# One more tile per batch multiplied with a whole table instead of gathered, and the softmax exponent of a slot moved behind a stretch of passes

## The chip, the cores and the metric

The kernel runs on one core of a Trainium2 chip, as one program. The metric is the device time of one execution in microseconds (us); lower is better. Engine names in the profile: PE is TensorE (PEld its weight loads), DVE is VectorE, ACT is ScalarE, POOL is GpSimd, SP is SyncE.

## The reference

For each of 16 batches of 512 tokens of width 128, a graph layer is followed by an attention layer with 8 heads, whose keys and values come from a memory of product keys. Per token and head, two similarity vectors over 128 sub-keys are cut to their top 16, their 256 sums again to the top 16, and the softmax of these weighs 16 rows of a table of 128 x 128 rows:

```
x = x + gnn(layernorm(x), adj)
q = x' @ Wq * D**-0.5                        # x' = layernorm(x)
scores, idx = top_k(sim, 16)                  # two sides of 128 keys
final_scores, pk_idx = top_k(all 256 sums, 16);  final_scores = softmax(final_scores)
k = einsum(final_scores, keys_table[ind]);  v = einsum(final_scores, values_table[ind])
out = softmax(causal(q k^T)) v;   x = x + concat(out) @ Wo
```

## The kernel before, in words

**Tiling.** A batch is 4 tiles of 128 tokens. Seven heads (`GH`) are gathered and one (`DENSE`, the eighth) is not. The work of a batch is laid out in 28 slots n = 4h + t, one per gathered head h and tile t. `schedule` runs a first batch, a loop of 14 and a last batch. Each engine has its own hand-ordered program over the same slots, tied by semaphores.

**A gathered tile.** DVE finds the rows (`rank`, `pairs_of`, `best_of`, `one_hot`, `hot_rows`, `sum_rows`, `even`, `lay`), always one head ahead and in pairs of tiles: `rank` for a pair in the slot with even t, the rest in the slot with odd t. At the end of that odd slot `take_laid` writes `rows` (L1131) and `spread`. POOL then issues 16 indirect DMAs for each tile (L397) into one of three buffers `got`. It waits for `rows_ready` and for `combined` of the tile three back. PE combines the rows with 32 matmuls (L659), which wait for the gathered rows. ACT copies the result to `kv` (L721, as all copies).

**The attention of the slot.** PE turns the keys (`key_transpose`, L544), ACT copies them, PE makes the scores (L548), DVE negates and masks them (`negate`, L1239), ACT takes the exponential (`exponent`, L826), PE turns the probabilities (`prob_transpose`, L554), ACT copies, PE multiplies with the values (L560), ACT copies, PE projects (L566), DVE adds (`add`, L1254, L1259).

**The dense head.** Its keys and values are made by multiplying a 128 x 16384 matrix of weights with the whole table. The matrix is built a piece at a time in *passes*. In a pass ACT makes four exponentials (`raise_`, L786), DVE cuts them by rank with four instructions (`weigh`, L1222), PE turns the four (`turn`, L506), ACT copies them (`take_wideT`), and PE multiplies (`multiply`, L520: four products, eight instructions in the trace). ACT is two passes ahead, DVE one, and `multiply` two behind `turn`. A pass serves 2 keys of 2 tiles, so two halves of 64 passes make 128 per batch. SP loads the table in chunks of 8 keys, 1 MB, into two buffers (`load_chunk`, L334); a chunk lasts 4 passes, and its load waits until the chunk two back is used up. Before chunk 5, SP stores the previous batch's output and waits until it has landed (L325, L327).

**Where the passes stand.** The plans `MIDDLE` (all batches but the last) and `ENDING` give each slot five counts, the passes of its five stretches. Stretch 3 and stretch 4 lie between scores and `prob_transpose` on PE; on ACT, `exponent` stands between them; stretch 5 comes before the values. Preparing a half of the dense head takes DVE four slots (`rank_dense`, `pairs_dense`, `best_dense`, `count_dense`, `norm_dense`; table `PREP`), and counting its ranks four *sets* of 16 instructions (`hit`, L1186) and of 16 PE matmuls (`add_hits`, L496), one slot each (table `HITS`), then `take_sum`. The dense head's own attention is interleaved in four slots.

**Order in a slot on ACT**, which the change touches:

```
k = passes(b, k, w[2], first, last)
exponent(slot, t)
k = passes(b, k, w[3], first, last)
take_probT(slot, t)
```

Of the kernel before, what the change touches and what calls it, by code (L numbers as in the profile page):

```python
# [21 lines left out]
SLOTS = GH * T  # L22
TOKENS = P // TOPK
# [6 lines left out]
HALF_PASSES = NKEYS // 2  # L30
PASSES = 2 * HALF_PASSES
CHUNK = 4
KEYS = 2 * CHUNK
CHUNKS = PASSES // CHUNK

# [15 lines left out]
ENDING = [  # L51
    FIVE, FOUR, FOUR, THREE,
    SEVEN, FIVE, SIX, FOUR,
    SEVEN, FIVE, SIX, FIVE,
    SEVEN, FIVE, SIX, FIVE,
    SIX, FIVE, SIX, FIVE,
    SEVEN, FIVE, SIX, FOUR,
    NONE, NONE, NONE, NONE]
# [7 lines left out]
PREP = {1: 0, 0: 20}  # L66
HITS = {1: {4: 0, 5: 1, 6: 2, 7: 3}, 0: {23: 0, 24: 1, 25: 2, 26: 3}}
# [24 lines left out]

def got_no(n):

    return n % 3 if n < SLOTS - 1 else 1


def got_back(n):

    return next(d for d in range(1, 6) if got_no((n - d) % SLOTS) == got_no(n))  # L100

# [15 lines left out]
def program(nc, x, adj, w_msg, w_upd, bias, wqpk_t, keys_t, wq, table, dense, wo, out):  # L117
# [85 lines left out]
    sim_d = sb("sim_d", [P, T, SIDES * NKEYS])  # L203
    top_v_d = sb("top_v_d", [P, 2, SIDES, TOPK])
# [9 lines left out]
    z_inv = sb("z_inv", [P, T])  # L214
    put = sb("put", [P, 2, SIDES, TOPK])
    hits = [sb(f"hits{i}", [P, TOPK, NKEYS], BF16) for i in range(2)]
    count_sb = sb("count_sb", [P, 2, NKEYS])
    rank1 = sb("rank1", [P, T, NKEYS])
    shift1 = sb("shift1", [P, T, NKEYS])
# [79 lines left out]

    def past(n):  # L300

        return max(n, 0) if isinstance(n, int) else n
# [13 lines left out]
    def _(sp):  # L316
# [48 lines left out]
    def _(pool):  # L365
# [19 lines left out]
        def batch(b, first=False, last=False):  # L385
            for n in range(SLOTS):
                h, t = n // T, n % T
                slot = b * SLOTS + n
                pool.wait_ge(rows_ready, slot + 1)
                pool.sem_inc(held, 1)  # L390

                if not (first and n < 3):
                    pool.wait_ge(combined, slot - (got_back(n) - 1))
                    pool.sem_inc(held, 1)
# [11 lines left out]
    def _(pe):  # L406
# [39 lines left out]
        def front(b, h, first=False, last=False):  # L446

            f = b * GH + h
            if h == 0:
                pe.wait_ge(xnT_copied, b * 2 + 2)  # L450
                pe.wait_ge(sim_d_copied, b * 2 + 1)
            elif h == 4 and not last:
                pe.wait_ge(xnT_copied, b * 2 + 3)
            elif h == 5 and not last:
                pe.wait_ge(x_used, b + 2)
            elif h == 2:
                pe.wait_ge(sim_d_copied, b * 2 + 2)
                if not first:
                    pe.wait_ge(added_d, b * 4)
            elif h == 3:  # L460
                pe.wait_ge(q_d_copied, b + 1)
            elif h == 6:
                pe.wait_ge(added_d, b * 4 + 2)
# [12 lines left out]
        def front_dense(b, half, f):  # L476
# [3 lines left out]
            for t in (2 * half, 2 * half + 1):  # L480
                last = pe.matmul(front_ps[1][:, (t % 2) * 256:(t % 2 + 1) * 256], x2nT[:, t * P:(t + 1) * P],
                                 w_sim[:, DENSE * 256:(DENSE + 1) * 256], start=True, stop=True)
# [7 lines left out]
        def add_hits(b, half, g):  # L490

            m = b * 8 + (half * 4 + g)
# [16 lines left out]
        def multiply(b, k):  # L509
            m = b * PASSES + k  # L510
            half, r = k // HALF_PASSES, k % HALF_PASSES
            if r % CHUNK == 0:
                c = k // CHUNK
                pe.wait_ge(tab_loaded[c % 2], b * (CHUNKS // 2 * 16) + (c // 2 + 1) * 16)
            if r == 0:
                pe.wait_ge(kv_d_copied, b * 4 + 2 * half)
            pe.wait_ge(wideT_copied, m + 1)
            for u in range(2):
                for v in range(2):
                    mm = pe.matmul(dense_ps[:, v * 2 * D:(v + 1) * 2 * D],  # L520
                                   wideT[k % 2][:, (2 * u + v) * P:(2 * u + v + 1) * P],
                                   tab[(k // CHUNK) % 2][:, (2 * k + u) % KEYS, :],
                                   start=(r == 0 and u == 0 and v == 0), stop=(r == HALF_PASSES - 1 and u == 1),
                                   skip_group_check=True)
# [15 lines left out]
        def key_transpose(a, t):  # L540
            pe.wait_ge(kv_copied, a + 1)
# [26 lines left out]
        def key_transpose_dense(c, tile, f):  # L568

            pe.wait_ge(kv_d_copied, c - tile + (tile // 2 * 2 + 2))  # L570
# [27 lines left out]
        def first():  # L598
# [17 lines left out]
            front_dense(0, 0, 0)  # L616
            for g in range(4):
                add_hits(0, 0, g)

        def batch(b, first=False, last=False):  # L620
            plan = ENDING if last else MIDDLE
            k = 0
            for n in range(SLOTS):
# [3 lines left out]
                if t == 0:  # L627
# [4 lines left out]
                    if h == 0:  # L632
                        front_dense(b, 1, b * GH + 1)
                    if h == GH - 2 and not last:
                        pe.wait_ge(q_copied, b * GH + GH)
                        transpose_xn(b * 2 + 3)
                        front_dense(b + 1, 0, b * GH + (GH - 1))
# [7 lines left out]
                end = last and n == SLOTS - 1  # L645
                if not end:
                    pe.wait_ge(gathered[t], s * (GATHERS * 16) + GATHERS * 16)
                pe.wait_ge(spread_ready, s * T + (T if t >= 2 else 2))
                pe.wait_ge(kv_copied, slot)

                sums = 4 + len([m for m in HITS[1] if m + 1 < n]) + (
                    0 if last else len([m for m in HITS[0] if m + 1 < n]))
                pe.wait_ge(sum_taken, b * 8 + sums)
                for c in range(PER_BAND):
                    if end:
                        pe.wait_ge(gathered_end[c], BANDS * 16)
                    for j in range(BANDS):
                        g = j * PER_BAND + c
                        mm = pe.matmul(comb_ps[j * BAND:(j + 1) * BAND, 0:2 * D],  # L659
                                       spread[:, t, j, c * BAND:(c + 1) * BAND],  # L660
                                       got[got_no(n)][:, g, :], start=(c == 0), stop=(c == PER_BAND - 1))
                mm.then_inc(combined, 1)
# [14 lines left out]
                key_transpose(slot, t)  # L677
# [3 lines left out]
                if tile is not None:  # L681
                    if n in LEFT:
                        pe.wait_ge(sim_d_copied, b * 2 + 2)
                    key_transpose_dense(c, tile, fronts(b, n, last))
                if n - 1 in HITS[1]:
                    add_hits(b, 1, HITS[1][n - 1])
                if n - 1 in HITS[0] and not last:
                    add_hits(b + 1, 0, HITS[0][n - 1])
# [30 lines left out]
    def _(act):  # L719
# [40 lines left out]
        def front_dense(b, half):  # L760
            act.wait_ge(sim_d_ready, b * 2 + (half + 1))
            copy(sim_d[:, 2 * half:2 * half + 2, :], front_ps[1][:, :]).then_inc(sim_d_copied, 1)
# [9 lines left out]
        def weights_dense(b, half):  # L772
            act.wait_ge(gap_d_ready, b * 2 + (half + 1))
            act.activation(wexp_d[:, :, :], gap_d[:, :, :], ACT.Exp).then_inc(wexp_d_ready, 1)

        def raise_(b, k):

            m = b * PASSES + k
            half = k // HALF_PASSES
            if k % HALF_PASSES == 0:  # L780
                act.wait_ge(shift_ready, b * 2 + (half + 1))
            act.wait_ge(wide_ready, past(m - 1))
            for u in range(2):
                for v in range(2):
                    key = (2 * k + u) % NKEYS
                    last = act.activation(expo[k % 2][:, 2 * u + v, :], sim_d[:, 2 * half + v, 0:NKEYS], ACT.Exp,  # L786
                                          bias=shift1[:, 2 * half + v, key:key + 1])
# [8 lines left out]
        def take_dense(b, half):  # L796
            act.wait_ge(dense_done, b * PASSES + (half + 1) * HALF_PASSES)
            act.wait_ge(z_ready, b * 2 + (half + 1))
            for v in range(2):
                t = 2 * half + v  # L800
                copy(kv_d[:, t, :], dense_ps[:, v * 2 * D:(v + 1) * 2 * D],
                     scale=z_inv[:, t:t + 1]).then_inc(kv_d_copied, 1)

        def passes(b, k0, count, first, last):
            for k in range(k0, k0 + count):
                if k == HALF_PASSES + 2:
                    take_dense(b, 0)
                if k == 2 and not first:
                    take_dense(b - 1, 1)
# [44 lines left out]
        def first():  # L854
# [11 lines left out]
            front_dense(0, 0)  # L866
            weights_dense(0, 0)
# [3 lines left out]
        def batch(b, first=False, last=False):  # L871
            plan = ENDING if last else MIDDLE
            k = 0
            for n in range(SLOTS):
# [3 lines left out]
                if t == 0:  # L878
# [4 lines left out]
                    if h == 0:  # L883
                        front_dense(b, 1)
                    if h == GH - 2 and not last:
                        gnn_out(b + 1)
                        front_dense(b + 1, 0)
                if n == 5:
                    query_dense(b)
                if last and n == SLOTS - 3:  # L890
                    take_wideT(b, PASSES - 1)
                    take_dense(b, 1)

                half, of_d, o = None, b, n - PREP[1]
                if o <= 6:
                    half = 1
                elif n >= PREP[0] and not last:
                    half, of_d, o = 0, b + 1, n - PREP[0]
# [4 lines left out]
                act.wait_ge(combined, slot + 1)  # L903
                copy(kv[:, t, :], comb_ps[:, 0:2 * D]).then_inc(kv_copied, 1)
# [547 lines left out]
```

## Time and profile before

| | |
|---|---|
| median of 3 runs | 9060.08 us (9057.7 to 9060.32) |
| the profiled execution, its own time | 9061.93 us |
| its span in the trace | 9060.0 us |
| mean granted TensorE clock | 0.926 |
| busy share PE, DVE, ACT, POOL | 83%, 76%, 54%, 75% |
| DMA | 1516.61 MB, mean 167 GB/s |

The span runs from the first to the last instruction. A busy share is an average over all stages. Idle time of an engine is put down to what ended it. A clock of 1.0 is 2.4 GHz and of 0.5 is 1.2 GHz; a mean between them is a mixture in time.

### The profile page before, as it was taken

The numbers are of one execution on the slowest core, as the hardware profiler recorded it, in microseconds if no ns is written. First come the engines' busy times: TensorE is split into PE (matmuls) and PEld (weight loads), VectorE is DVE, ScalarE is ACT, GpSimd is POOL, SyncE is SP. The second block draws the span as 40 slices with busy tenths as digits, with TensorE's granted clock in tenths as the row PEclk, the third lists the DMA queues.
The fourth block names the chain that finished last, engine by engine and source line by source line (L and its number), as shares of the span: only waits on it lengthen the run. The fifth ranks groups of instructions, "written<-read, shape, count | busy, mean of one in ns | idle before, by whom it ended". The sixth has DMA issues, their size and how long they took to land.

```text
span 9060.0 us, 175549 instructions
## 1 busy us (share of the span) xinstructions
PE 7538.4 (83%) x49440; PEld 5845.8 (65%) x49440; DVE 6929.1 (76%) x30876; ACT 4869.8 (54%) x14163; POOL 6800.1 (75%) x7179
## 2 busy tenths in 40 slices
PE   5888888888888888888888888888888888788887
PEld 4666666666666666666666666666666666666675
DVE  7777777777877778777777777777777777777775
ACT  3555555555555555555555555555555555555564
POOL 5777777777777777777777777777777777777777
PEclk8999999999999999999999899999999999999998
DMA  4555555555555555555555555555555555555554
GB/s 135 170 172 167 166 169 171 168 172 164 171 166 172 168 166 170 170 168 171 165 170 166 168 171 166 170 170 171 167 163 173 171 169 170 168 168 166 165 178 146
DMA packets 445968, 1516.61 MB, mean 167 GB/s; under 512 B 123760, under 2 KB 141552, under 8 KB 379248
## 3 DMA queue, kind: packets, MB, share of 16 engines
q0 software_dynamic: 344064, 939.98, 34.0%
q1 hardware_dynamic: 100848, 564.37, 17.8%
q8 instruction: 441, 7.23, 0.3%
q14 instruction: 615, 5.04, 0.2%
HBM read 1499.66 MB, written 4.19 MB: 166 GB/s over the span
## 4 chain that ended last, share of the span: by engine, by line
POOL 62%; issue 21%; PE 8%; DVE 5%; DMA 2%; ACT 1%; POOLq 0%; DVEq 0%; ACTq 0%
POOL got L397 62%; PE dense_ps L520 3%; DMA got<-in_table,rows 2%; PE comb_ps L659 2%; DVE wide L1222 1%; PE wideT_ps L506 1%; DVE chosen L1103 0%; PE front_ps L469 0%; DVE onehot L1098 0%; DVE onehot L1091 0%; ACT expo L786 0%; DVE hits L1186 0%; PE score_ps L560 0%; PE comb_ps L496 0%; PE score_ps L548 0%
## 5 line engine op out<-in xcount | busy, mean ns | idle before, releaser
L397 POOL DMA_INDIRECT got<-in_table,rows x7168 | 6797.4, 948 | 2243.0 <-issue 2155.6
L520 PE MATMUL dense_ps<-tab,wideT 128*128 128x256 f32 x16384 | 4058.6, 392 | 3.2 <-ACT kv_d L721 2.5
L520 PEld LDWEIGHTS dense_ps<-tab,wideT 128*128 128x128 f32 x16384 | 3072.8, 196 | 700.5 <-issue 313.7
L1222 DVE SCALAR_TENSOR_TENSOR wide<-const_ps,rank,expo 128x128 f32<-128x128 f32 x8192 | 2304.2, 345 | 1595.7 <-PE wideT_ps L506 1282.5
L786 ACT ACTIVATE expo<-sim_d,shift 128x128 f32<-128x128 f32 x8192 | 2596.3, 392 | 76.0 <-DVE wide L1222 74.0
L659 PE MATMUL comb_ps<-got,spread 128*32 128x256 f32 x14336 | 1160.9, 479 | 1071.9 <-DMA got<-in_table,rows 1022.2
L721 ACT ACTIVATE wideT<-wideT_ps 128x512 f32<-128x512 f32 x2048 | 1212.1, 592 | 1163.2 <-PE wideT_ps L506 1162.3
L659 PEld LDWEIGHTS comb_ps<-got,spread 128*32 128x32 f32 x14336 | 529.8, 131 | 1561.9 <-issue 766.2
L506 PE MATMUL wideT_ps<-ident,wide 128*128 128x128 f32 x8192 | 1241.8, 274 | 179.9 <-ACT wideT L721 154.8
L506 PEld LDWEIGHTS wideT_ps<-ident,wide 128*128 128x128 f32 x8192 | 987.1, 142 | 381.3 <-issue 183.2
L721 ACT ACTIVATE kv<-comb_ps 128x256 f32<-128x256 f32 x448 | 170.3, 380 | 1338.4 <-PE comb_ps L659 1337.4
L1186 DVE TENSOR_SCALAR hits<-iota_b,top_f_d,put 128x128 bf16<-128x128 bf16 x2048 | 519.1, 339 | 2.8 <-DVE z_inv L1197 0.2
L826 ACT ACTIVATE prob<-neg,neg_max 128x128 f32<-128x128 f32 x448 | 250.8, 560 | 370.3 <-DVE neg_max L1239 368.0
L1091 DVE TENSOR_TENSOR onehot<-place,const_ps 128x1600 f32<-128x1600 uint32 (+1 forms) x225 | 407.1, 1810 | 0.0
L1098 DVE TENSOR_TENSOR onehot<-onehot,const_ps 128x1600 f32<-128x1600 f32 (+1 forms) x225 | 406.3, 1806 | 0.1
L1103 DVE TENSOR_REDUCE chosen<-onehot 128x32 f32<-128x1600 f32 (+1 forms) x225 | 405.8, 1803 | 0.0
L560 PEld LDWEIGHTS score_ps<-probT,kv 128*128 128x128 f32 x2240 | 318.7, 194 | 78.5 <-ACT probT L721 58.1
L560 PE MATMUL score_ps<-probT,kv 128*128 128x128 f32 x2240 | 333.8, 280 | 39.4 <-ACT probT L721 39.4
L548 PE MATMUL score_ps<-keyT,qT 128*128 128x512 f32 (+3 forms) x896 | 348.1, 470 | 13.3 <-ACT keyT L721 13.1
L721 ACT ACTIVATE keyT<-probT_ps 128x128 f32<-128x128 f32 x448 | 118.2, 264 | 327.0 <-PE probT_ps L544 327.0
L1239 DVE CUSTOM_DVE_ANT_0 neg<-score_ps,mask 128x128 f32<-128x128 f32 x448 | 217.5, 485 | 98.9 <-PE score_ps L548 51.9
L721 ACT ACTIVATE probT<-probT_ps 128x128 f32<-128x128 f32 x448 | 194.1, 433 | 177.5 <-PE probT_ps L554 174.1
(169 smaller groups left out, 6793.8 us busy)
## 6 DMA issues: line engine op xcount, KB each, us to landing
tab<-in_dense SPq DMA_DIRECT2D x512, 1024.0 KB
got<-in_table,rows POOLq DMA_INDIRECT x7168, 2.7
adj_i<-in_adj SPq DMA_DIRECT2D x16, 1024.0 KB
x_in<-in_x SPq DMA_DIRECT2D x16, 256.0 KB, 5.9
out<-fin SPq DMA_DIRECT2D x16, 256.0 KB, 6.7
tab<-in_wqpk_t SPq DMA_DIRECT2D x1, 512.0 KB, 10.9
tab<-in_keys_t SPq DMA_DIRECT2D x1, 512.0 KB, 15.2
wq_sb<-in_wq SPq DMA_DIRECT2D x1, 512.0 KB, 14.3
```

What stands on the lines that cost most here:

```text
L397: pool.indirect_dma_start(out=got[got_no(n)][:, g, :], out_offset=None, in_=table, in_offset=bass.IndirectOffsetOnAxis(ap=rows[:, t * GATH ...
L506: mm = pe.transpose(wideT_ps[:, q * P:(q + 1) * P], wide[k % 2][:, q, :], ident[:, :])
L520: mm = pe.matmul(dense_ps[:, v * 2 * D:(v + 1) * 2 * D], wideT[k % 2][:, (2 * u + v) * P:(2 * u + v + 1) * P], tab[(k // CHUNK) % 2][:, (2 ...
L560: last = pe.matmul(headT_ps, kv[:, j, D:2 * D], probT[:, j * P:(j + 1) * P], start=(j == 0), stop=(j == t))
L659: mm = pe.matmul(comb_ps[j * BAND:(j + 1) * BAND, 0:2 * D], spread[:, t, j, c * BAND:(c + 1) * BAND], got[got_no(n)][:, g, :], start=(c == ...
L721: return act.activation(dst, src, ACT.Copy, scale=scale)
L786: last = act.activation(expo[k % 2][:, 2 * u + v, :], sim_d[:, 2 * half + v, 0:NKEYS], ACT.Exp, bias=shift1[:, 2 * half + v, key:key + 1])
L1091: after(link(dve.tensor_tensor(onehot[:, 0:nt, :, :].rearrange("p t k c -> p (t k) c"), place[:, t0:t0 + nt, :].rearrange("p t k -> p (t k ...
L1098: after(link(dve.tensor_tensor(hot, hot, cand[:, 0:nt, 1, :].unsqueeze(2).broadcast_to([P, nt, TOPK, NCAND]), ALU.mult)))
L1103: link(dve.tensor_reduce(chosen[:, 0:nt, 0, :], onehot[:, 0:nt, :, :], AX.X, ALU.add))
L1186: last = dve.tensor_scalar(hits[g % 2][:, a, :], iota_b[:, :], top_f_d[:, u, side, a:a + 1], put[:, u, side, a:a + 1], ALU.is_equal, ALU.mult)
L1222: last = dve.scalar_tensor_tensor(wide[k % 2][:, 2 * u + v, :], count_ps[:, v, :], rank1[:, 2 * half + v, key:key + 1], expo[k % 2][:, 2 * ...
```

## The change

Tile 3 of head 4 (slot 19, `EXTRA_SLOT`) is no longer gathered. Its keys and values come from passes over the whole table of head 4 (a new input `extra`), with 4 keys of the one tile in a pass: 32 passes, so a batch has three groups LOW (tiles 0, 1 of the dense head), ALONE (the new one) and HIGH (tiles 2, 3), and 160 passes. 27 tiles are gathered. Its group has its own preparation (slots 0 to 3, for one tile), two sets of `hit` (slots 3, 4), and its result is copied straight to `kv`. HIGH is prepared in slots 6 to 9, its sets lie in slots 10, 12, 14 and 15. A chunk of the table lasts 2 passes in ALONE. POOL leaves slot 19 out, and `got` is now used in strict turn. The plans are written anew. On ACT `exponent` (and `exponent_dense`) stands behind the fourth stretch. `weigh` waits at each group's start for its own last product.

```diff
+EXTRA, EXTRA_TILE = 4, T - 1
+EXTRA_SLOT = EXTRA * T + EXTRA_TILE
+TILES = SLOTS - 1
...
-HALF_PASSES = NKEYS // 2
-PASSES = 2 * HALF_PASSES
-CHUNK = 4
-KEYS = 2 * CHUNK
-CHUNKS = PASSES // CHUNK
+LOW, ALONE, HIGH = range(3)
+KEYS = 8
+PASS_KEYS = {LOW: 2, ALONE: 4, HIGH: 2}
+COLUMNS = {LOW: (0, 1), ALONE: (4,), HIGH: (2, 3)}
...
+PASSES = END[HIGH]
+GROUP_CHUNKS = NKEYS // KEYS
+CHUNKS = 3 * GROUP_CHUNKS
...
+EIGHT = (2, 2, 1, 2, 1)
 MIDDLE = [
-    FIVE, THREE, FIVE, FIVE,
-    FIVE, THREE, SIX, THREE,
-    FIVE, FIVE, SIX, FIVE,
-    FIVE, FOUR, FOUR, FIVE,
-    FIVE, FOUR, FIVE, FIVE,
-    FIVE, FOUR, FIVE, THREE,
-    FIVE, THREE, FIVE, FIVE]
+    SEVEN, FIVE, SIX, FOUR,
+    SEVEN, SIX, SIX, FIVE,
+    SIX, FIVE, SIX, SIX,
+    SIX, FIVE, FIVE, FIVE,
+    SEVEN, SIX, SEVEN, SEVEN,
+    SIX, FIVE, FIVE, FOUR,
+    SIX, FOUR, SEVEN, SIX]
...
-PREP = {1: 0, 0: 20}
-HITS = {1: {4: 0, 5: 1, 6: 2, 7: 3}, 0: {23: 0, 24: 1, 25: 2, 26: 3}}
+PREP = {0: ALONE, 6: HIGH, 20: LOW}
+HITS = {3: (ALONE, 0), 4: (ALONE, 1),
+        10: (HIGH, 0), 12: (HIGH, 1), 14: (HIGH, 2), 15: (HIGH, 3),
+        23: (LOW, 0), 24: (LOW, 1), 25: (LOW, 2), 26: (LOW, 3)}
...
         def load_chunk(b, c, first=False):
-            if not (first and c < 2):
-                sp.wait_ge(dense_done, b * PASSES + (c - 1) * CHUNK)
-            k = (c % (CHUNKS // 2)) * KEYS
-            sp.dma_start(tab[c % 2][:, :, :], dense[:, k:k + KEYS, :]).then_inc(tab_loaded[c % 2], 16)
+            if c >= 2:
+                sp.wait_ge(dense_done, b * PASSES + chunk_end(c - 2))
+            elif not first:
+                sp.wait_ge(dense_done, b * PASSES - (PASSES - chunk_end(c + CHUNKS - 2)))
+            k = (c % GROUP_CHUNKS) * KEYS
+            source = extra if c // GROUP_CHUNKS == ALONE else dense
+            sp.dma_start(tab[c % 2][:, :, :], source[:, k:k + KEYS, :]).then_inc(tab_loaded[c % 2], 16)
...
@@ pool
+                if n == EXTRA_SLOT:
+                    continue
+                tile = b * TILES + gathers(n)
+                pool.wait_ge(rows_ready, tile + 1)
...
@@ scalar
                 k = passes(b, k, w[2], first, last)
...
+                k = passes(b, k, w[3], first, last)
                 exponent(slot, t)
                 if tile is not None:
                     exponent_dense(c, tile)
-                k = passes(b, k, w[3], first, last)
                 take_probT(slot, t)
...
@@ vector
         def weigh(b, k):
             m = b * PASSES + k
-            half = k // HALF_PASSES
-            if k % HALF_PASSES == 0:
-                after(link(dve.tensor_copy(count_ps, count_sb[:, :, :])))
+            j = group(k)
+            if k == BEGIN[j]:
+                dve.wait_ge(wide_ready, past(m))
+                dve.sem_inc(held, 1)
+                after(link(dve.tensor_copy(count_ps[:, 0:len(COLUMNS[j]), :], counts(j))))
```

## Rows read from the trace of the kernel before

**Rows 1.** The page, busy time of each engine, whole run.
```profile
PE 7538.4 (83%) x49440; PEld 5845.8 (65%) x49440; DVE 6929.1 (76%) x30876; ACT 4869.8 (54%) x14163; POOL 6800.1 (75%) x7179
```

**Rows 2.** The page, the chain of work that ended last, by engine.
```profile
POOL 62%; issue 21%; PE 8%; DVE 5%; DMA 2%; ACT 1%; POOLq 0%; DVEq 0%; ACTq 0%
```

**Rows 3.** Waits of POOL, whole run: us in total, times, longest us.
```profile
POOL got L397 <- issue: 2155.6, 7076, 0.3
POOL got L397 <- DVE rows L1131: 60.3, 24, 43.8
POOL got L397 <- PE comb_ps L659: 27.1, 68, 6.7
```

**Rows 4.** Line L397's instructions: ns min/median/max, first and last start.
```profile
L397 POOL DMA_INDIRECT got<-in_table,rows x7168: 942/946/1316, 47.1 to 9042.7; - x200
```

**Rows 5.** Window of one batch: engines' busy time (instructions), clock, DMA share, GB/s.
```profile
5137.30:5698.00 560.70, 472.24 (x3080) 367.45 (x3080) 431.14 (x1925) 303.62 (x884) 424.27 (x448) 0.92 0.53 169
```

**Rows 6.** Waits of PE in that batch (smaller ones left out).
```profile
PE comb_ps L659 <- DMA got<-in_table,rows: 51.4, 17, 5.5
PE wideT_ps L506 <- ACT wideT L721: 13.9, 8, 5.1
PE comb_ps L659 <- DVE spread L1138: 9.5, 2, 6.3
PE front_ps L469 <- issue: 3.7, 1, 3.7
```

**Rows 7.** Waits of DVE in that batch (smaller ones left out).
```profile
DVE wide L1222 <- PE wideT_ps L506: 78.2, 23, 9.7
DVE acc L1259 <- PE probT_ps L566: 10.7, 6, 4.4
DVE wide L1222 <- ACT expo L786: 4.9, 10, 1.5
```

**Rows 8.** Timeline of PE: a pass, a set, combines and stalls at both clock levels.
```profile
5095.81 3.64 PE L659 MATMUL comb_ps<-got,spread 128*32 128x256 f32 x32 [5.00 <-DMA got<-in_table,rows]
...
5124.94 1.06 PE L496 MATMUL comb_ps<-hits,ident_b 128*128 128x128 bf16 x16
...
5140.99 3.77 PE L469 MATMUL front_ps<-w_sim,x2nT 128*128 128x256 f32 x8 [3.67 <-issue]
...
5147.19 1.93 PE L659 MATMUL comb_ps<-got,spread 128*32 128x256 f32 x32
...
5194.71 1.09 PE L506 MATMUL wideT_ps<-ident,wide 128*128 128x128 f32 x4 [3.30 <-ACT wideT L721]
...
5212.72 1.89 PE L520 MATMUL dense_ps<-tab,wideT 128*128 128x256 f32 x8
5214.45 0.60 PE L506 MATMUL wideT_ps<-ident,wide 128*128 128x128 f32 x4
5214.89 0.60 PE L554 MATMUL probT_ps<-ident,prob 128*128 128x128 f32 x4
...
5221.65 0.64 PE L659 MATMUL comb_ps<-got,spread 128*32 128x256 f32 x8
```

**Rows 9.** The costliest groups of the run: DVE's work for passes and sets.
```profile
L1222 DVE SCALAR_TENSOR_TENSOR wide<-const_ps,rank,expo 128x128 f32<-128x128 f32 x8192 | 2304.2, 345 | 1595.7 <-PE wideT_ps L506 1282.5
L1186 DVE TENSOR_SCALAR hits<-iota_b,top_f_d,put 128x128 bf16<-128x128 bf16 x2048 | 519.1, 339 | 2.8 <-DVE z_inv L1197 0.2
```

**Rows 10.** Timeline of ACT in slots 2 and 3 of that batch.
```profile
5192.66 0.62 ACT L826 ACTIVATE prob<-neg,neg_max 128x384 f32<-128x384 f32 x1 [2.07 <-DVE neg_max L1239]
...
5193.99 0.57 ACT L721 ACTIVATE wideT<-wideT_ps 128x512 f32<-128x512 f32 x1
...
5212.38 0.72 ACT L826 ACTIVATE prob<-neg,neg_max 128x512 f32<-128x512 f32 x1 [0.71 <-DVE neg_max L1239]
5213.01 0.19 ACT L826 ACTIVATION_READ_ACCUMULATOR prob<-neg,neg_max 128x1 f32 x1
5213.11 0.57 ACT L721 ACTIVATE wideT<-wideT_ps 128x512 f32<-128x512 f32 x1
5213.58 1.27 ACT L786 ACTIVATE expo<-sim_d,shift 128x128 f32<-128x128 f32 x4
```

**Rows 11.** Windows behind a table load that SP issued at 5217.25.
```profile
5218.00:5224.00 6.00, 6.00 (x51) 3.66 (x50) 5.32 (x16) 3.71 (x10) 4.54 (x5) 1.00 0.80 274
5224.00:5230.00 6.00, 6.00 (x34) 5.19 (x34) 6.00 (x33) 3.93 (x12) 4.48 (x6) 1.00 0.36 102
```

**Rows 12.** Timeline, rows written just before the next combine.
```profile
4533.86 0.25 DVE L1131 SCALAR_TENSOR_TENSOR rows<-turned,upper,half 128x32 uint32<-128x32 f32 x1
...
4534.52 3.64 PE L659 MATMUL comb_ps<-got,spread 128*32 128x256 f32 x32 [6.14 <-DMA got<-in_table,rows]
```

**Rows 13.** Timeline of POOL while DVE stands idle at the run's end.
```profile
9018.99 0.95 POOL L397 DMA_INDIRECT got<-in_table,rows  x1 [0.30 <-issue]
9020.24 0.95 POOL L397 DMA_INDIRECT got<-in_table,rows  x1 [0.30 <-issue]
```

More of the change, by code:

```diff
@@ L90, in buf, with gathers, tiles_before, pair @@
     return 2 if h == GH - 1 else h % 2
+def gathers(n):
+    return n - (n > EXTRA_SLOT)
 def got_no(n):
-    return n % 3 if n < SLOTS - 1 else 1
-def got_back(n):
-    return next(d for d in range(1, 6) if got_no((n - d) % SLOTS) == got_no(n))
+    return gathers(n) % 3
+def tiles_before(b, h):
+    if h == GH:
+        return tiles_before(b + 1, 0)
+    return b * TILES + (h * T - (h > EXTRA))
+def pair(t, h):
+    t0, nt = PAIRS[t // 2]
+    return t0, nt - (h % GH == EXTRA and t0 + nt == T)
 def dense_tile(b, n, first, last):
@@ L298, in program, with sims @@
     held = sem("held")
+    def sims(j):
+        return [sim_x[:, :]] if j == ALONE else [sim_d[:, t, :] for t in COLUMNS[j]]
     def past(n):
@@ L642, in batch @@
                     multiply(b, PASSES - 1)
[L645 to L662, printed above, removed]
+                if n != EXTRA_SLOT:
+                    end = last and n == SLOTS - 1
+                    if not end and t == EXTRA_TILE:
+                        pe.wait_ge(gathered[t], (b * (GH - 1) + (h - (h > EXTRA)) + 1) * (GATHERS * 16))
+                    elif not end:
+                        pe.wait_ge(gathered[t], s * (GATHERS * 16) + GATHERS * 16)
+                    t0, nt = pair(t, h)
+                    pe.wait_ge(spread_ready, tiles_before(b, h) + (t0 + nt))
+                    pe.wait_ge(kv_copied, b * TILES + gathers(n))
+                    sums = 4 + len([m for m in HITS if m + 1 < n and hits_of(0, m, last)])
+                    pe.wait_ge(sum_taken, b * ALL_SETS + sums)
+                    for c in range(PER_BAND):
+                        if end:
+                            pe.wait_ge(gathered_end[c], BANDS * 16)
+                        for j in range(BANDS):
+                            g = j * PER_BAND + c
+                            mm = pe.matmul(comb_ps[j * BAND:(j + 1) * BAND, 0:2 * D],
+                                           spread[:, t, j, c * BAND:(c + 1) * BAND],
+                                           got[got_no(n)][:, g, :], start=(c == 0), stop=(c == PER_BAND - 1))
+                    mm.then_inc(combined, 1)
@@ L682, in batch @@
                     if n in LEFT:
[L683 to L688, printed above, removed]
+                        pe.wait_ge(sim_d_copied, b * 3 + 2)
+                    key_transpose_dense(of, c, tile, fronts(b, n, last))
+                if hits_of(b, n - 1, last):
+                    add_hits(*hits_of(b, n - 1, last))
                 k = passes(b, k, w[1], first)
@@ L794, in take_wideT, with take_dense @@
             copy(wideT[k % 2][:, :], wideT_ps[:, :]).then_inc(wideT_copied, 1)
[L796 to L801, printed above, removed]
+        def take_dense(b, j):
+            act.wait_ge(dense_done, b * PASSES + END[j])
+            act.wait_ge(z_ready, b * 3 + (j + 1))
+            for v, t in enumerate(COLUMNS[j]):
+                copy(kv[:, EXTRA_TILE, :] if j == ALONE else kv_d[:, t, :], dense_ps[:, v * 2 * D:(v + 1) * 2 * D],
                      scale=z_inv[:, t:t + 1]).then_inc(kv_d_copied, 1)
@@ L891, in batch @@
                     take_wideT(b, PASSES - 1)
[L892 to L898, printed above, removed]
+                    take_dense(b, HIGH)
+                group_d, of_d, o = prep(b, n, last)
                 tile, of = dense_tile(b, n, first, last)
@@ L920, in batch @@
                 if t in (1, 3) and not (last and h == GH - 1):
-                    weights((s + 1) * T, *PAIRS[t // 2])
-                if half is not None and o == 2:
-                    weights_dense(of_d, half)
+                    weights(tiles_before(b, h + 1), *pair(t, h + 1))
+                if o == 2:
+                    weights_dense(of_d, group_d)
+                k = passes(b, k, w[3], first, last)
                 exponent(slot, t)
@@ L1367, in batch @@
                 k = passes(b, k, w[2], last)
[L1368 to L1372 removed]
+                if hits_of(b, n - 1, last):
+                    take_sum(*hits_of(b, n - 1, last))
+                negate(slot, n)
                 if tile is not None:
@@ L1397, in batch @@
                     hot_rows(nt)
-                if half is not None and o == 0:
-                    rank_dense(of_d, half, 1)
+                if o == 0:
+                    rank_dense(of_d, group_d, 1)
                 k = passes(b, k, w[4], last)
@@ L1404, in batch @@
                     lay(nt)
-                if half is not None and o == 0:
-                    rank_dense(of_d, half, 2)
+                if o == 0:
+                    rank_dense(of_d, group_d, 2)
                 final = h == GH - 1 and (last or t < 2)
```

327 lines of the change are left out of this document (184 added, 143 removed).

## The prediction

> **What bounds the kernel now.** I read the page first. POOL is busy for only 75% of the span, less than PE (83%) and DVE (76%) [rows 1], yet the chain that ended last runs through POOL for 62% and through "issue" for 21% [rows 2]. The waits of POOL join the two: 2155.6 us of its idle time are 0.3 us before each indirect DMA in which it waited for nothing, and rows and buffers cost it 87.4 us, half of that before the first gather [rows 3]. So one gather costs 0.948 + 0.30 = 1.25 us, a tile of 16 of them 19.98 us, and a batch of 28 tiles 559.6 us. Line L397 says the same: 7168 starts from 47.1 to 9042.7 [rows 4]. The stretch from 5137.3 to 5698.0 is one batch of the loop, 560.7 us [rows 5]. In it PE waits 51.4 us for gathered rows and 9.5 for `spread` [rows 6], and DVE 78.2 us for PE [rows 7]. **POOL is the bound, with PE and DVE some 60 us a batch behind it.** The question is whether they stay behind once POOL has 20 us less and they have more.
>
> **POOL.** It loses 16 gathers a batch, 19.98 us. 27 tiles take 539.6 us. If nothing else decided, the time would be the profiled execution's 9061.9 - 16 x 19.98 = 8742 us. (That execution lies 1.9 us above the median of the runs, so I read the sums as they are.)
>
> **A new wait of POOL.** Rows for tiles 0 and 1 of head 5 are written at the end of slot 17. Until now POOL still had two tiles to gather by then, 18 and 19; now only 18. The rows show how tight this is. `rows` was written at 4533.86, and ready at 4534.1; the combine behind it started at 4534.52 on gathers that POOL had issued at least 2.7 us earlier (issue to landing, the page) [rows 12]. So POOL would have stood 2.3 us at that place, more if DVE is late. I take 3 us a batch (0 to 20). And PE must then do slots 18 and 19 while one tile is gathered: it falls a slot behind and has the rest of the batch to catch up.
>
> **PE.** In the batch it is occupied 472.2 us [rows 5], waits 61 us at the combine, and 27 us for other things. A pass costs 2.17 us at 2.4 GHz (from 5212.72 to 5214.89: eight product instructions, then four turns) [rows 8]. 32 more make 69.4 us. Two more sets add 0.9 to 1.06 us each [rows 8], one combine goes (1.93), the fronts change by 0.5: together +70. Against this the clock. It is granted at 0.92 in this batch [rows 5], that is at 1.2 GHz for 16% of the time, 90 us. A combine behind an idle time of 5.00 us took 3.64 us, one behind no idle time 1.93 [rows 8]. If PE works through these 90 us, half is lost. When gathers are no longer waited for, most of that comes back: 0 to 45 us, I take 35, since the seventeen waits for gathers are the commonest idle time, and the 3.67 us at the loop's jump stays [rows 8].
>
> **ScalarE's exponent.** Now ACT can't copy `wideT` while `exponent` waits for DVE. At 5192.66 it had waited 2.07 us, its next copy came at 5193.99 [rows 10], and PE stood 3.30 us for it [rows 8]. Such waits are 13.9 us a batch [rows 6]. They go, since by the end of the fourth stretch the scores have long been negated. What comes instead is late probabilities: behind `turn` of the last pass but one, ACT now has a copy (0.57), four exponentials (1.27), the probabilities (0.72) and their sum (0.19) [rows 10], 2.75 us with 0.1 to 0.2 for signals, while PE reaches `prob_transpose` in 2.17. That is 0.6 to 0.8 us a slot with t = 3 and less below. 28 of these are at most 22 us; in half of the slots PE has time anyway, so 11. Net 27 - 14 + 11 = 24.
>
> PE's sum is 472 + 70 - 35 + 24 = **531 us**, with ends at 510 (whole clock back, no exposure) and 577 (no clock back, all exposed).
>
> **DVE.** Busy 431.1; of its 129.6 us idle 93.8 are waits for PE and ACT [rows 7], so 35.8 are its own gaps: 467 us. 128 more `weigh` instructions at 2304.2/8192 = 0.281 us are 36.0, 32 more `hit` instructions at 519.1/2048 = 0.253 are 8.1 [rows 9]. The preparation of one tile moves from the gathered to the dense side at about equal cost; I cost it at nothing, 3 us either way. **511 us**, with ends 508 and 516.
>
> **Table loads.** In ALONE a chunk lasts two passes, 4.3 us back to back. A load takes about 6: SP issued at 5217.25, the DMA engines were busy to 0.80 until 5224 and back at 0.36 behind it [rows 11]. Sixteen chunks could cost 1.7 us each, 27 us. But the plan spreads 32 passes over six slots, 7 us a chunk, with stretches of one or two passes; I take 2 us and keep 27 for the range. Bandwidth has room: 274 GB/s stood in the loaded window, while 1 MB in 7 us and the gathers make some 250. Chunk 5 also stands in SP's queue behind the store. The store waits for the end of slot 2; 7 us for it and 6 for the chunk are 13, and pass 20 is multiplied only in slot 4: hidden by all of slot 3.
>
> **Sum.** POOL 540, PE 531, DVE 511. None can be simply on top: slots with odd t are heavy on DVE (three 1.8 us steps of `one_hot`), slots with t = 0 on PE (the next head's front), and each pass ties the two. POOL's buffers absorb about a slot of lag, not more. I put 3 us for the rows and 4 for such crossings on top of 540: **547 us a batch**. 9061.9 - 16 x (560.7 - 547) = 8843 us.
>
> **A rule that speaks against it.** POOL's issues take 942 ns at least and 946 in the median [rows 4]; at the run's end, with DVE idle, they take 950 and come 1.25 us apart [rows 13], as in the middle. By these rows DVE's work doesn't slow POOL. The Trainium skill, "SBUF — State Buffer", "SBUF: two separate sides", states that DVE operations in certain modes hold a port that GpSimd needs to write the descriptors of its DMAs, which then wait. By that rule the sum would grow with DVE's work; by the row it doesn't, and the row decides here.
>
> **Rivals.**
>
> *POOL alone (8742 to 8790).* The waits of PE and DVE vanish into slack and only the rows cost something. For it: the sums 531 and 511 lie below 540. Against it: a margin of 9 us over 28 slots is thin when slots are uneven.
>
> *PE and DVE together (8900 to 9040).* Slots 0 to 3 of this batch waited for no gather: from the combine at 5147.19 to that at 5221.65 they took 74.5 us for 18 passes [rows 8], 18.6 us a slot, though PE alone needed far less. Four more passes there, at DVE's price of 1.1, make 79 us; seven such groups are 553 us a batch, 8939 us.
>
> *Slower (9100 to 9300).* The same place, with the four passes at PE's price: 74.5 + 8.7 = 83.2, because DVE and PE wait in turn in each slot and neither hides the other's. Not all groups are so bad; with half of them so and the others at POOL's 80, which is 81.6 a group, a batch is 571 us and the time 9227. It decides from a mean slot of 560.7/28 = 20.02 us on. Against it: the 3.30 us stall in that stretch is one that the moved exponent removes.
>
> *The port.* Were POOL held by DVE's added 44 us, a batch would be 540 + 44 = 584 and the time 9435 us. No row shows it.
>
> *No net effect.* POOL's 20 us are given back whole as waits for rows in the slots around 19: 9062.
>
> **Numbers.** The forecast 8843, with its own range 8790 to 8900, gets 0.42; POOL alone 0.2; PE and DVE together 0.18; no effect 0.06; slower 0.13; the port 0.01. A measurement of this kernel can tell about 0.2%, 18 us, from no change. Faster is 0.42 + 0.2 + 0.18 = 0.80, same 0.06, slower 0.14. The range starts at POOL's bound, 8742, and goes to 9080, beyond the second rival and no effect.
>
> **What would show it.** In the changed profile: L397 with 6912 gathers at 946 ns; a batch of 547 us; a wait of POOL for `rows` of 2 to 6 us once a batch; PE's waits for gathers below 20 us a batch and the clock above 0.96; PE's waits for ACT's `wideT` below 3 us and for `prob` from nothing to some 10. I am wrong if POOL waits for rows by more than 15 us a batch (then the pair of PE and DVE is the bound), or if the clock stays at 0.92.

## The result and the profile after

The changed kernel takes 9200.63 us (median of 4 runs, 9194.21 to 9204.14) against 9060.07 before. The ratio is 1.0155 with a 95% interval of 1.0137 to 1.0173: 1.6% slower, where 2.4% faster was forecast. The profiled execution has a span of 9198.8 us and a mean granted clock of 0.98.

The page of the changed kernel, the busy time of the engines [rows 1]:

```profile
PE 8415.5 (91%) x55616; PEld 6685.5 (73%) x55616; DVE 7587.2 (82%) x33772; ACT 5774.4 (63%) x16755; POOL 6550.9 (71%) x6923
```

Its chain of work that ended last, by engine [rows 2]:

```profile
PE 48%; DVE 30%; ACT 10%; issue 7%; POOL 2%; DMA 1%; DVEq 1%; ACTq 0%; POOLq 0%
```

Before, POOL and "issue", with the 0.3 us ahead of each gather in it, made 83% of the chain; now POOL is 2% of it and "issue" 7%. Its waits over the whole run [rows 3], and its instructions [rows 4]:

```profile
POOL got L481 <- issue: 2114.8, 6817, 1.5
POOL got L481 <- DVE rows L1225: 505.7, 92, 43.2
POOL got L481 <- PE comb_ps L752: 12.2, 3, 7.5
```

```profile
L481 POOL DMA_INDIRECT got<-in_table,rows x6912: 940/946/1152, 46.5 to 9183.2; - x198
```

A gather costs what it did, and 256 of them are gone. But POOL now waits some 460 us for rows after its first gather (505.7 in all, less the 43.2 before the first one).

One batch, from one loop jump to the next (columns as in [rows 5]):

```profile
4081.90:4651.70 569.80, 525.06 (x3475) 416.91 (x3474) 473.42 (x2110) 361.05 (x1047) 409.27 (x433) 0.99 0.59 192
```

The waits of PE in that batch [rows 6]:

```profile
PE probT_ps L642 <- ACT prob L921: 13.4, 24, 1.3
PE probT_ps L632 <- ACT kv L812: 9.9, 13, 2.4
PE wideT_ps L592 <- DVE wide L1325: 7.7, 5, 3.1
PE probT_ps L654 <- ACT headT L812: 4.0, 5, 0.8
PE front_ps L554 <- issue: 3.6, 1, 3.6
PE wideT_ps L592 <- ACT wideT L812: 1.5, 3, 0.7
```

PE is busy for 525 of 569.8 us and waits for no gather in this batch (3.7 us in the whole run). The waits of PE over the whole run, the largest and those that the experiments move:

```profile
PE probT_ps L642 <- ACT prob L921: 210.0, 383, 1.8
PE probT_ps L632 <- ACT kv L812: 165.0, 216, 3.6
PE wideT_ps L592 <- DVE wide L1325: 114.9, 75, 3.2
PE probT_ps L654 <- ACT headT L812: 59.3, 77, 0.9
...
PE wideT_ps L592 <- ACT wideT L812: 22.0, 44, 0.7
```

**A batch takes 9.1 us longer than the 560.7 us it took when POOL set the pace. What sets it now is the chain through PE and the engines that serve it, DVE and ACT: 88% of the path.**

### The profile page after: what moved, and what is told of

It is laid out like the page before. It is cut to its first block, busy times and chain, and to the rows that moved or that the text cites. A ratio compares the mean times of both kernels' runs of the same rounds, so it can differ in the third digit from the quotient of the medians.

```text
span 9198.8 us, 197626 instructions
## 1 busy us (share of the span) xinstructions
PE 8415.5 (91%) x55616; PEld 6685.5 (73%) x55616; DVE 7587.2 (82%) x33772; ACT 5774.4 (63%) x16755; POOL 6550.9 (71%) x6923
## 4 chain that ended last, share of the span: by engine, by line
PE 48%; DVE 30%; ACT 10%; issue 7%; POOL 2%; DMA 1%; DVEq 1%; ACTq 0%; POOLq 0%
PE dense_ps L606 22%; DVE wide L1325 10%; ACT expo L880 7%; PE wideT_ps L592 6%; PE comb_ps L752 6%; DVE hits L1284 3%; POOL got L481 2%; DVE onehot L1185 2%; PE front_ps L554 2%; DVE onehot L1192 2%; DVE chosen L1197 2%; PE score_ps L648 2%; ACT prob L921 2%; PE score_ps L636 2%; PE probT_ps L642 1%
## 5 line engine op out<-in xcount | busy, mean ns | idle before, releaser
L481 POOL DMA_INDIRECT got<-in_table,rows x6912 | 6548.1, 947 | 2632.7 <-issue 2114.8
L606 PE MATMUL dense_ps<-tab,wideT 128*128 128x256 f32 x20480 | 4972.9, 387 | 11.2 <-DMA tab<-in_extra 9.2
L606 PEld LDWEIGHTS dense_ps<-tab,wideT 128*128 128x128 f32 x20480 | 3773.5, 193 | 700.0 <-issue 232.3
L1325 DVE SCALAR_TENSOR_TENSOR wide<-const_ps,rank,expo 128x128 f32<-128x128 f32 x10240 | 2863.1, 344 | 999.7 <-PE wideT_ps L592 697.5
L812 ACT ACTIVATE wideT<-wideT_ps 128x512 f32<-128x512 f32 x2560 | 1521.8, 594 | 1787.1 <-PE wideT_ps L592 1782.4
L592 PE MATMUL wideT_ps<-ident,wide 128*128 128x128 f32 x10240 | 1556.4, 275 | 138.6 <-DVE wide L1325 114.9
L592 PEld LDWEIGHTS wideT_ps<-ident,wide 128*128 128x128 f32 x10240 | 1233.8, 142 | 368.1 <-DVE wide L1325 157.6
L752 PE MATMUL comb_ps<-got,spread 128*32 128x256 f32 x13824 | 857.1, 389 | 3.7 <-DMA got<-in_table,rows 3.7
L880 ACT ACTIVATE expo<-sim_x,shift 128x128 f32<-128x128 f32 x2048 | 649.7, 392 | 134.1 <-DVE wide L1325 133.9
L642 PE MATMUL probT_ps<-ident,prob 128*128 128x128 f32 x1120 | 228.1, 303 | 214.2 <-ACT prob L921 210.0
## 6 DMA issues: line engine op xcount, KB each, us to landing
tab<-in_keys_t SPq DMA_DIRECT2D x1, 512.0 KB, 13.4
```

What stands on the lines that cost most here:

```text
L481: pool.indirect_dma_start(out=got[got_no(n)][:, g, :], out_offset=None, in_=table, in_offset=bass.IndirectOffsetOnAxis(ap=rows[:, t * GATH ...
L592: mm = pe.transpose(wideT_ps[:, q * P:(q + 1) * P], wide[k % 2][:, q, :], ident[:, :])
L606: mm = pe.matmul(dense_ps[:, v * 2 * D:(v + 1) * 2 * D], wideT[k % 2][:, q * P:(q + 1) * P], tab[c % 2][:, key % KEYS, :], start=(begins a ...
L752: mm = pe.matmul(comb_ps[j * BAND:(j + 1) * BAND, 0:2 * D], spread[:, t, j, c * BAND:(c + 1) * BAND], got[got_no(n)][:, g, :], start=(c == ...
L812: return act.activation(dst, src, ACT.Copy, scale=scale)
L880: last = act.activation(expo[k % 2][:, q, :], sims(j)[v][:, 0:NKEYS], ACT.Exp, bias=shift1[:, COLUMNS[j][v], key:key + 1])
```

## The experiments

Each ratio is to the kernel before, run on the same chip. The changed kernel's is 1.0155. Where a time is split below, "busy" and "waits" are PE's in the profiled execution; the busy time of one kind of instruction is counted from the trace as the time in which no earlier one still ran.

**1. The exponent back, in the changed kernel.**

```diff
-                k = passes(b, k, w[3], first, last)
                 exponent(slot, t)
                 if tile is not None:
                     exponent_dense(c, tile)
+                k = passes(b, k, w[3], first, last)
```

> The changed kernel with the exponent back before the fourth stretch of passes on ScalarE; all else as changed. Theory 1 (TensorE's own work bounds the changed kernel: 525 us busy and 45 us of small waits in a batch of 570 us): the 13.4 us a batch in which it waited for the probabilities go, and up to 14 us of waits for ScalarE's copy of wideT come back, so within 0.6% of the changed kernel's 9200 us, 9150 to 9260. Rival (the moved exponent is what made it slower): back to 9060 or below.

9152.42 us, ratio 1.0103 (1.0086 to 1.012). At the lower edge of theory 1, and far from 9060: the moved exponent did not make the kernel slow, but in this kernel it costs 0.5% rather than giving anything. The waits of PE, whole run:

```profile
PE wideT_ps L592 <- ACT wideT L812: 297.3, 182, 5.0
PE probT_ps L632 <- ACT kv L812: 217.9, 216, 3.7
...
PE wideT_ps L592 <- DVE wide L1325: 7.3, 15, 0.6
PE probT_ps L642 <- ACT prob L921: 3.2, 3, 1.8
```

The waits for `wideT` came back, and those for the probabilities and for DVE's cuts (114.9 to 7.3 us) went. In all PE waits as long as in the changed kernel (790.2 against 783.3 us). What is shorter is its busy time, 8345.0 against 8415.5 us for the same instructions, and that lies on the turns of the probabilities (`prob_transpose`) behind the wait: 132.9 us against 227.7, of which the lower clock (0.975 against 0.980) takes a part back.

**2. The exponent moved, in the kernel before.** The same edit in the other direction.

> The kernel before with only the exponent moved behind the fourth stretch. Theory (GpSimd's gathers bound it, TensorE has 60 us a batch to spare): no change, 9045 to 9070 us, waits for ScalarE's wideT near nothing and waits for the probabilities of about 10 us a batch in their place. Rival (the late probabilities lie on the path): 9100 or more.

9058.47 us, ratio 1.0001 (0.9991 to 1.001). Where POOL sets the pace, the place of the exponent is worth nothing. Its waits of PE, whole run:

```profile
PE comb_ps L659 <- DMA got<-in_table,rows: 918.5, 310, 8.0
PE probT_ps L554 <- ACT prob L826: 147.1, 352, 1.8
...
PE wideT_ps L506 <- ACT wideT L721: 23.7, 31, 0.8
```

The waits are exchanged as it was reasoned: 154.8 us for `wideT` became 23.7, and 147.1 us for the probabilities took their place. But the exchange isn't even. The turns of the probabilities behind those waits grew from 128.1 to 224.4 us of busy time, and the waits for gathers, 1022.2 us before, paid for it.

**3. Work of the new group taken from TensorE, then from VectorE, then from both.** In the new group's 32 passes three of four products are left out:

```diff
-            for q, (key, v) in enumerate(units(k)):
+            for q, (key, v) in enumerate(units(k)[:1] if j == ALONE else units(k)):
                 mm = pe.matmul(dense_ps[:, v * 2 * D:(v + 1) * 2 * D], wideT[k % 2][:, q * P:(q + 1) * P],
...
-                               stop=(ends and q >= 4 - len(COLUMNS[j])), skip_group_check=True)
+                               stop=(ends and (j == ALONE or q >= 4 - len(COLUMNS[j]))), skip_group_check=True)
```

> The changed kernel, leaving out three of the four products of each pass of the new group (96 products of 0.43 us, 41 us of TensorE a batch); VectorE, ScalarE, turns and table loads as changed. Theory 1: the batch falls from 570 us by most of 41 us to GpSimd's 540 us or little above, 8740 to 8880. Theory 2: VectorE holds it, at most 10 us a batch less, 9040 to 9200.

9046.1 us, ratio 0.9983 (0.9974 to 0.9993): 154 us less, 10 us a batch out of 41, within the range of theory 2. Theory 1 in its plain form is out: the new products are not simply on the path. PE's busy time fell by 472 us and its waits rose by 320: those for DVE's cuts from 114.9 to 207.7, for the probabilities to 259.6, for `wideT` to 71.5. The granted clock fell too, from 0.980 to 0.962: PE was busy for 554 us at 1.2 GHz, 261 us more than in the changed kernel. If half of such time is lost, that ate 131 us of the relief (an estimate). The same edit on the loop of `weigh`:

> The changed kernel, leaving out three of the four cuts by rank (VectorE) of each pass of the new group: 96 instructions of 0.281 us, 27 us of VectorE a batch. Theory 1: TensorE waited 7.7 us a batch for VectorE's cuts in all, in the new group's part of the batch less than half of that, so 9120 to 9200. Theory 2: most of 27 us a batch, 8770 to 8900.

9122.36 us, ratio 1.0065 (1.0048 to 1.0082): 78 us less, as theory 1 had it. VectorE's order alone is not the bound either. Both edits together:

> The changed kernel, leaving out three of the four products on TensorE and three of the four cuts on VectorE of each pass of the new group. Alone these gave 154 and 78 us. Theory 3 (in each slot TensorE and VectorE wait for each other in turn, so that the one's relief is taken up by the other): more than their sum, 8750 to 8900 us. Rival (they bound different slots): the sum, 8950 to 8990.

9052.97 us, ratio 0.9992 (0.9983 to 1.0002). Neither theory expected this: the two together give no more than the products alone. That contradicts theory 3, by which each engine's relief was eaten by the other. PE's waits for the cuts fell again, from 207.7 to 119.1 us, but waits for gathers (15.5 us with the products alone) took their place. The whole-run waits of PE and POOL in this kernel:

```profile
PE comb_ps L752 <- DMA got<-in_table,rows: 116.9, 44, 6.0
```

```profile
POOL got L481 <- DVE rows L1225: 331.2, 117, 41.5
```

PE waits for gathers again, while POOL waits for rows: both in one batch, at different places. In one batch (PE's from 4026 us on) PE waited 3.1 and 2.4 us for gathers in slots 16 and 17, and POOL 7.5 us for rows behind slot 18.

**4. POOL given its 20 us back.** Eight small loads, each waited for, in slot 19.

```diff
                 if n == EXTRA_SLOT:
+                    for i in range(8):
+                        pool.dma_start(spin[:, :], x[0, 0:P, :]).then_inc(spun, 16)
+                        pool.wait_ge(spun, b * 128 + (i + 1) * 16)
+                        pool.sem_inc(held, 1)
                     continue
```

> The changed kernel in which GpSimd has its 20 us of slot 19 back: it makes 8 small loads one after the other, each waited for (2.4 us or so each), into a buffer nobody reads. Theory 1 or 3 (GpSimd isn't the bound after the change; it stands 28 us a batch for rows, 19 of them in one place behind slot 18): no change, 9180 to 9220 us, that wait of 19 us shrinking to nothing. Rival (GpSimd's waits for rows are a part of the path): 16 x 20 us more, 9500.

9234.08 us, ratio 1.0189 (1.0172 to 1.0206). In the trace the loads took (69.8 + 365.5)/16 = 27 us a batch, 435 us in all; the kernel became 33 us longer, more than the "no change" expected and far less than the rival's 320.

```profile
POOL got L487 <- DVE rows L1231: 84.0, 55, 41.5
```

The 505.7 us of waits for rows went down to 84.0, and PE's waits for gathers rose from 3.7 to 60.9. **What the change takes from POOL is worth next to nothing once PE is late.** The wait it replaces is this one, in the changed kernel's timeline of POOL:

```profile
4433.92 0.95 POOL L481 DMA_INDIRECT got<-in_table,rows  x1 [0.30 <-issue]
4453.86 0.94 POOL L481 DMA_INDIRECT got<-in_table,rows  x1 [18.99 <-DVE rows L1225]
```

**5. ScalarE's last exponentials held back.** The trace of the changed kernel shows how PE comes to wait for `kv` and the probabilities. PE, then ACT, in slot 8:

```profile
4252.71 1.89 PE L606 MATMUL dense_ps<-tab,wideT 128*128 128x256 f32 x8
4254.99 0.33 PE L632 MATMUL probT_ps<-ident,kv 128*128 128x128 f32 x1 [0.39 <-ACT kv L812]
```

```profile
4252.91 0.60 ACT L812 ACTIVATE wideT<-wideT_ps 128x512 f32<-128x512 f32 x1 [1.99 <-PE wideT_ps L592]
4253.40 1.26 ACT L880 ACTIVATE expo<-sim_d,shift 128x128 f32<-128x128 f32 x4
4254.57 0.36 ACT L812 ACTIVATE kv<-comb_ps 128x256 f32<-128x256 f32 x1
```

The combine was done at 4250.5, but a copy of `wideT` and four exponentials, which are needed only two passes later, stand ahead of the copy to `kv`. The edit keeps back the last `raise_` of a stretch until the attention step behind it is issued: `hold=True` makes `passes` keep it, and the new `flush()` issues it. Here for the fourth stretch (the lines inside `passes` are left out):

```diff
-                k = passes(b, k, w[3], first, last)
+                k = passes(b, k, w[3], first, last, hold=True)
                 exponent(slot, t)
                 if tile is not None:
                     exponent_dense(c, tile)
+                flush()
```

At the exponent only:

> The changed kernel, but on ScalarE the exponent stands ahead of the last pass's four exponentials of the fourth stretch, and behind its copy of wideT. Theory 1: TensorE's waits for the probabilities (13.4 us a batch) shrink below 2 us and nothing takes their place: 16 x 12 us less, 9000 to 9060. Theory 2 (VectorE's in-order work bounds the batch): those waits only move to another place, 9170 to 9210.

9111.33 us, ratio 1.0056 (1.0039 to 1.0072): 89 us less. Less than theory 1 expected: the waits for probabilities fell from 210.0 to 38.0 us, those for `kv` and `headT` grew from 165.0 to 206.7 and 59.3 to 89.8. It is also faster than run 1, which had the exponent in its old place (1.0056 against 1.0103). At `kv` only:

> The changed kernel with only the last four exponentials of the first stretch held behind ScalarE's copy of kv. Theory 4 (TensorE is the bound, and a late answer of ScalarE costs it time wherever it stands): its waits for kv, 165 us in all, go and half or more comes through, 9050 to 9120 us. Rival (all three places are needed, since a wait taken away in one comes back in the next): 9170 or more.

Ratio 1.0038 (1.0024 to 1.0052), 9109.45 us where the kernel before took 9075.33: 1.2% below the changed kernel, as theory 4 had it. But its waits fell by only 18 us in all: 162.5 us of waits for `kv` went, and those for the probabilities rose to 260.1 and for the cuts to 175.8. The larger part is busy time, 73 us less, 52 of it on the turns of the keys behind `kv` (105.2 to 52.8). At all three places:

> The changed kernel with the last four exponentials of a stretch put behind the attention step that follows, in three places on ScalarE: behind the copy of kv, behind the exponent, behind the copy of headT. Theory 1 (TensorE's chain with its small waits on ScalarE): the first run of this kind took 172 us of waits for probabilities away and gained 89; here some 200 us more (kv 207, headT 90 in that run) go, half of it comes through: 8960 to 9050 us. Rival (VectorE's order decides): 9090 or more.

**8923.77 us, ratio 0.985 (0.9833 to 0.9866), faster than both kernels** and more than was expected. One batch of it, and its whole-run waits of PE:

```profile
3959.70:4512.70 553.00, 516.34 (x3473) 414.94 (x3473) 472.51 (x2105) 356.98 (x1044) 408.38 (x432) 0.99 0.60 198
```

```profile
PE wideT_ps L592 <- DVE wide L1336: 258.1, 211, 3.2
PE probT_ps L642 <- ACT prob L929: 68.8, 100, 1.8
```

The batch fell from 569.8 to 553.0 us. Over the run PE waits 146 us less than in the changed kernel and is busy 132 us less. Waits for VectorE's cuts (258.1, 114.9 in the changed kernel) are now the largest. With the exponent back and the other two places late:

> The changed kernel with the exponent back before the fourth stretch, and the four exponentials held behind the copies of kv and of headT. Theory 4: against the kernel with all three places late (8924 us), ScalarE's copy of wideT again stands behind a wait for VectorE's negated scores, which was 297 us of TensorE's waits in the run with the exponent back alone: 8980 to 9080 us. Rival (the exponent's place makes no difference once its exponentials are late): 8900 to 8950.

Ratio 0.9942 (0.9925 to 0.9958), 9022.22 us: 0.9% behind the kernel with all three late. The waits for `wideT` are 435.4 us. So the moved exponent is right, but only with its last exponentials behind it. The exponentials held at `kv` and `headT` in the kernel before, its exponent where it was:

> The kernel before with the exponentials held behind the copies of kv and headT, all else as before. Theory (GpSimd bounds the kernel before): no change, 9045 to 9070 us, so that the gain of 1.5% needs the gathered tile's removal as well. Rival (late answers cost the kernel before too): 9000 or less.

Ratio 1.0001 (0.9991 to 1.001), 9076.43 us against 9075.33 of the kernel before in that session. Neither this nor run 2 gains anything there; all three places at once were not tried in the kernel before. As far as these two runs show, the gain of 1.5% needs the gathered tile's removal and ScalarE's order together.

**6. All three late, and one product of four.** The edits of 3 (products) and 5 together.

> The kernel with all three places late, leaving out three of four products of each pass of the new group, as in an earlier run where this gave 154 us. Theory 5 (TensorE's own work bounds it in slots 18 to 10, and in slots 11 to 17 it soon meets GpSimd's gathers): again only part of 41 us a batch, 8800 to 8870 us, with TensorE waiting for gathers about slots 15 to 17 and GpSimd for rows behind slot 18. Rival (nothing but TensorE's sum counts): GpSimd's floor, 8742 to 8780.

8906.0 us, ratio 0.9813 (0.9797 to 0.9829). Only 0.4% below the kernel of run 5; the time is above what theory 5 had, but its two signs are there. One batch, two of PE's four waits for gathers in it, and the one long wait of POOL:

```profile
4100.00:4650.00 550.00, 488.41 (x3283) 382.94 (x3282) 472.49 (x2109) 356.90 (x1048) 410.15 (x432) 0.96 0.59 199
```

```profile
4286.62 3.59 PE L752 MATMUL comb_ps<-got,spread 128*32 128x256 f32 x32 [2.58 <-DMA got<-in_table,rows]
4306.45 1.93 PE L752 MATMUL comb_ps<-got,spread 128*32 128x256 f32 x32 [0.65 <-DMA got<-in_table,rows]
```

```profile
4310.94 0.95 POOL L481 DMA_INDIRECT got<-in_table,rows  x1 [8.41 <-DVE rows L1236]
```

PE catches up with POOL's gathers in slots 13 to 18, and then nothing more can be won there. Behind slot 18 POOL still waits 8.4 us for the rows of head 5, although PE now runs at the pace of the gathers. With all its waits for rows POOL's own batch is 541 + 9 = 550 us, and this kernel's batch takes about 550: POOL has no slack left in it. That rows can't come earlier in this layout is argued, not shown. This also accounts for a part of run 3: in slots 11 to 17, where the new group lies, relief carries only as far as the gathers (116.9 us of waits with both edits). With the products alone it was spent before that, on waits for DVE and ACT and on the clock. Here too the granted clock fell, from 0.982 to 0.957.

## Why the prediction was wrong

**What was right.** POOL bounded the kernel before: neither reordering of ScalarE changes its time (1.0001 both). A gather costs what it cost: 946 ns in the median again, and the mean went from 948 to 947 ns with DVE busy for 9.5% longer. So the trace shows nothing of the stall that the Trainium skill's "SBUF — State Buffer", "SBUF: two separate sides", describes, as the prediction weighed it. Whether a DVE instruction of this kernel runs in such a mode, no run here tells. DVE's busy time of a batch came to 473.4 us, 42 more than in [rows 5]; the two terms gave 44. The clock rose to 0.99, as expected above 0.96. The table loads were hidden: 9.2 us of waits in all, less than the 2 us a batch put in. And the sign that was named for being wrong, POOL waiting for rows by more than 15 us a batch, is the one that showed: 28.4 us in the batch above.

**The step that failed is PE's sum**, 531 us, set below POOL's 540, by which POOL stayed the bound. Measured: 569.8, of which 525.1 busy and 44.7 waiting. Both parts were too small, by 18 us and by 21.

*The waits* were put at 24 us. The probabilities cost 13.4, where 11 stood, and `wideT` 1.5. What was not in the sum is what comes when PE no longer stands at the combine: 9.9 us for `kv`, 4.0 for `headT`, and 7.7 for DVE's cuts (1.6 in the batch of [rows 5], 23.5 us in the whole run before). As I read it, PE's 61 us a batch of waiting at the combine, in 19 of 28 slots, had let ACT and DVE catch up. I carried the 27 us of other waits over as if they were a property of those steps. Run 5 shows that they decide: taking ACT's late answers away gives 277 us, from 1.6% slower to 1.5% faster, 146 us in waits and 132 in busy time.

*The busy part* was put at 472 + 70 - 35 = 507 us. It is 525. The trace gives two reasons of about 9 us each. The first is the clock's term. I let PE work through all of the 90 us at 1.2 GHz and then took back 35 of 45. In the batch of [rows 5] the clock was at 1.2 GHz for 85.3 us, and PE was already busy for 69.2 of them; in the changed kernel's batch it still is for 17.0. Half of the difference, 26 us, is what the clock gave back (an estimate). The second is that a wait isn't free in busy time either. In the same two batches the turns of the probabilities took 14.1 us instead of 8.3 and those of the keys 6.5 instead of 3.7, with the same number of instructions: a turn that doesn't have to wait starts while the matmuls ahead of it still run, and a turn behind a wait finds none. Run 5's best kernel shows the same from the other side. It has the same matrix instructions and nearly the same clock (0.982 against 0.980), yet 8283.2 us busy against 8415.5, 8 us a batch less. On the turns of probabilities and keys and the projections behind them lie 138 us less.

**The exponent** was booked at -14 + 11. The two kinds of wait were right in size, and run 2 shows them exchanged. The sign was wrong: 0.5% worse in the changed kernel. Two terms were at nothing. The waits for `wideT` that went, 275 us, were in part replaced by waits for DVE's cuts (7.3 us with the exponent in its old place, 114.9 with it moved), and the turns behind the waits for probabilities, which stood in 24 of 28 slots, took 95 us more busy time, 6 us a batch.

**The rivals.** The time lies in the range of the slower rival (9100 to 9300, chance 0.13), and a mean slot of 569.8/28 = 20.35 us is beyond its point of 20.02. Its mechanism, TensorE and VectorE waiting in turn so that neither hides the other, holds only in part: then taking work from both had to give more than the sum, and it gave no more than one. ScalarE's order was what was missing in it. The second rival's group of four slots, 79 us for 22 passes, was nearer to the truth than the sums of the engines. The same four slots took 79.3 us in the changed kernel, and the next three groups 78.9, 79.8 and 80.6. The last three are uneven, 88.1, 73.0 and 90.3, so that seven make 570. That rival rested on the only four slots in a row of its batch that waited for no gather, and I gave it 0.18. That the slower rival's own 81.6 us a group comes so near the measured mean of 81.4 is luck: the groups are not half at 83.2 and half at 80.

**POOL's new wait** was put at 3 us, with 20 as the upper end. The one wait behind slot 18 was 19 us in the changed kernel (28.4 with the others of the batch), nearly all of it off the path (run 4), and 8.4 in the kernel where POOL has no slack (run 6).

## What to carry to other kernels

When the engine that sets the pace is relieved, don't add the new work to the others' busy time and their old waits: their small waits can be short because they had slack, so take the price from stretches of the trace in which they didn't wait for the old bound. On an in-order engine that serves another, put the work that is needed later (here exponentials for two passes on) behind the answer that is needed now; in this kernel that was worth 3%, and nothing, in the two places tried, while another engine was the bound. Price a wait with what follows it: the instruction behind it loses its overlap as well. Skipping one step of a steady stream also moves the stream's next inputs forward by a step, and their producer may not be ready.

## What the runs showed that I had not expected

Relief doesn't add: products alone gave 154 us, cuts alone 78, both together 148. On top of the held exponentials, the same relief of the products was worth 0.4%, not 1.7%. And an engine's busy time depends on the waits in it: the same 55616 matrix instructions were 8415.5 us busy in one order of ScalarE and 8283.2 in another, at nearly the same clock.
